# A click model on one core: two half chunks first, ten gathers a chunk, layer 0 of six chunks one group later

## The reference

```python
z0 = einsum('bid,bjd->bdij', x0, x0).reshape(B, D, F0 * F0)
cur0 = relu(einsum('bdk,kl->bld', z0, W0))            # 128 rows
next_h, direct0 = split(cur0, 2, axis=1)              # 64 and 64
z1 = einsum('bid,bjd->bdij', x0, next_h).reshape(B, D, F0 * 64)
cur1 = relu(einsum('bdk,kl->bld', z1, W1))            # 128 rows
z = sum(concat([direct0, cur1], axis=1), axis=-1)     # over d
h = relu(concat([z, dense_ctx]) @ W_top1 + b_top1)
h = relu(h @ W_top2 + b_top2);  y = h @ W_top3
```

## Time and profile before

| | us |
|---|---|
| median of three runs | 443.81 |
| the profiled run | 441.91 |
| span of its trace (first to last instruction) | 439.9 |
| PE busy | 407.8 |
| DVE busy | 347.9 |
| ACT busy | 225.7 |
| POOL busy | 285.5 |

### The profile page before, as it was taken

How to read it: one execution, slowest core, us unless ns; L and a number is a source line. 1 busy time by engine, 2 the same in 40 slices (tenths; PEclk the granted TensorE clock), 3 DMA queues, 4 the chain that set the end, 5 groups by cost and what they waited for, 6 DMA issues and landing times.

```text
span 439.9 us, 4140 instructions
## 1 busy us (share of the span) xinstructions
PE 407.8 (93%) x1490; PEld 250.4 (57%) x1490; DVE 347.9 (79%) x196; ACT 225.7 (51%) x224; POOL 285.5 (65%) x180
## 2 busy tenths in 40 slices
PE   0578699899999999999999999999999999996997
PEld 0444356446566656565756565666656565664564
DVE  0203755799999998989898989898989898999700
ACT  3114345365565647483747474747383747462422
POOL 5787878888888888888888888888888100000000
PEclk9989799999999999999999999999999999999899
DMA  8373629696959495959595977777786858570000
GB/s 282 97 180 76 133 62 217 155 208 153 213 116 213 111 208 112 212 110 216 108 220 120 200 142 171 157 178 153 176 165 157 180 138 197 127 161 0 1 0 2
DMA packets 23988, 64.03 MB, mean 146 GB/s; under 512 B 6755, under 2 KB 14904, under 8 KB 17695
## 3 DMA queue, kind: packets, MB, share of 16 engines
q1 hardware_dynamic: 17620, 60.75, 61.7%
q0 software_dynamic: 5632, 1.35, 3.1%
q10 hardware_dynamic: 715, 1.66, 1.1%
HBM read 59.88 MB, written 3.85 MB: 145 GB/s over the span
## 4 chain that ended last, share of the span: by engine, by line
PE 76%; POOL 12%; issue 5%; DVE 3%; DMA 3%; ACT 0%; DVEq 0%
PE acc L487 15%; POOL found L266 12%; PE acc L519 12%; PE acc L512 11%; PE acc L511 11%; PE acc L530 9%; PE sums L470 6%; PE acc L526 4%; PE spread L500 3%; DVE z_lo L409 3%; DMA found<-in_table_dram,rows_sb 2%; PE spread L559 2%; PE sums L550 1%; DVE z L401 1%; DMA base_sb<-in_base_dram 1%
## 5 line engine op out<-in xcount | busy, mean ns | idle before, releaser
L266 POOL DMA_INDIRECT found<-in_table_dram,rows_sb x176 | 285.3, 1621 | 56.7 <-issue 53.3
L309 ACT ACTIVATE z_hi<-z 128x2048 fp32r<-128x2048 f32 x64 | 122.4, 1912 | 83.1 <-DVE z L401 78.4
L409 DVE TENSOR_TENSOR z_lo<-z,z_hi 128x2048 fp32r<-128x2048 f32 x64 | 146.2, 2286 | 14.6 <-ACT z_hi L309 8.8
L487 PE MATMUL acc<-squares,w 128*128 128x512 f32 (+1 forms) x224 | 111.2, 614 | 0.0
L511 PE MATMUL acc<-z_hi,w_hi 128*128 128x512 f32 x256 | 106.2, 415 | 4.5 <-issue 2.3
L401 DVE TENSOR_TENSOR z<-x_wide,h 128x2048 f32<-128x2048 f32 x48 | 109.6, 2283 | 0.0
L512 PE MATMUL acc<-z_hi,w_lo 128*128 128x512 f32 x256 | 100.2, 391 | 0.0
L401 DVE TENSOR_TENSOR z<-spread,h 128x2048 f32<-128x2048 f32 x32 | 73.2, 2286 | 20.8 <-issue 17.0
L285 ACT ACTIVATE squares<-sums 128x1024 f32<-128x1024 f32 x64 | 58.4, 913 | 59.7 <-PE sums L470 45.7
L519 PE MATMUL acc<-z_lo,w_hi 128*128 128x512 f32 x256 | 83.3, 447 | 1.8 <-DVE z_lo L409 1.8
L519 PEld LDWEIGHTS acc<-z_lo,w_hi 128*128 128x128 f32 x256 | 48.5, 191 | 26.2 <-issue 15.1
(11 more groups left out here) (44 smaller groups left out, 144.5 us busy)
## 6 DMA issues: line engine op xcount, KB each, us to landing
x_wide<-x_rows SPq DMA_DIRECT2D x96, 512.0 KB
x_parts<-x_rows SPq DMA_DIRECT2D x32, 128.0 KB
found<-in_table_dram,rows_sb POOLq DMA_INDIRECT x176
x_rows<-found SPq DMA_DIRECT2D x32, 80.4 KB
w_sb<-in_w_dram SPq DMA_DIRECT2D x1, 1280.0 KB, 6.8
x_rows<-found SPq DMA_DIRECT2D x16, 73.1 KB
z<-in_select_dram ACTq DMA_DIRECT2D x1, 576.0 KB, 7.5
wt_sb<-in_wt_dram SPq DMA_DIRECT2D x1, 512.0 KB
```

The costliest lines, as they stand in the source:

```text
L266: pool.indirect_dma_start(out=found[:, b, 2, s * D:s * D + D], out_offset=None, in_=table, in_offset=bass.IndirectOffsetOnAxis(ap=rows_sb[ ...
L309: nc.scalar.activation(z_hi[:, n % RING], z[:, n % RING], ACT.Copy).then_inc(hi_done, 1)
L409: nc.vector.tensor_tensor(z_lo[:, n % RING], z[:, n % RING], z_hi[:, n % RING], ALU.subtract).then_inc(lo_done, 1)
L487: last = nc.tensor.matmul(acc0[:, :], w0[rows, t, :], squares[rows, q % RING0, a, :], start=(t == 0), stop=(t == T0 - 1))
```

## The change

- 17 chunks: two of 16 samples (256 columns), then fifteen of 32. Every instruction takes the width of its chunk.
- Gathers fetch rows in the order in which they lie in `x_rows`, 125 partitions at a time: five for the half chunks, ten for the others (160 instead of 176). The table starts are added per entry, so `base_sb` is as large as `ids_sb`. The rows go out in one transfer of 125 partitions instead of three of 39.
- The weights are loaded in another order, those of the MLP only after chunk 4's rows; `split` of chunk 0 comes earlier on ACT and DVE; the filler matmuls (`keep_busy`) are placed otherwise, and 16 stand ahead of chunk 2.
- Layer 0 of chunk c + 1 for chunks from 7 on: first sum at the end of group 4 of chunk c - 1, the next steps in groups 0, 1 and 2 of chunk c, the last contraction beside the f32 group. For chunks in `LATE` (1 to 6): first sum at the end of group 0 of chunk c, the next in groups 1 to 3, the last contraction after the high matmuls of group 3, and `h` is evicted behind it. Their `split` stands at g = 4 of chunk c - 1, on DVE behind the low part; for the others at g = 2. Chunk 2 is an exception: most of its layer 0 stands alone at the end of chunk 1, where the low part of group 4 goes ahead of the next multiply.
- On SP the way through DRAM (`bring`) of chunk c + 2 stands among the `widen` of chunk c + 1.
- The MLP of the early samples stands in groups 3 and 4 of the last chunk instead of 2 to 4.

Left out are the lines in which only the width changes.

```diff
 F = 39
 D = 16
 HALF = 64
-CB = 32
-N = CB * D
-CHUNKS = B // CB
-SETS = 3
-GP = SETS * F
-SLOTS = -(-CB // SETS)
-GW = SLOTS * D
-SET_COLS = [GW, GW, N - 2 * GW]
+
+SIZES = [16, 16] + [32] * 15
+CHUNKS = len(SIZES)
+START = [sum(SIZES[:c]) for c in range(CHUNKS)]
+WIDTH = [size * D for size in SIZES]
+N = max(WIDTH)
+
+GP = 125
+SLOTS = [-(-F * size // GP) for size in SIZES]
+SLOT0 = [sum(SLOTS[:c]) for c in range(CHUNKS)]
+GW = max(SLOTS) * D
 DENSE = 16
...
+LATE = range(1, 7)
...
-        ids_sb = sb("ids_sb", [GP, CHUNKS * SLOTS], I32)
-        base_sb = sb("base_sb", [GP, 1])
-        rows_sb = sb("rows_sb", [GP, CHUNKS * SLOTS], U32)
+        ids_sb = sb("ids_sb", [GP, sum(SLOTS)], I32)
+        base_sb = sb("base_sb", [GP, sum(SLOTS)], I32)
+        rows_sb = sb("rows_sb", [GP, sum(SLOTS)], U32)
         found = sb("found", [GP, BUFS, 3, GW])
-        x_rows = nc.dram_tensor("x_rows", (BUFS, 3, FR, N), F32, kind="Internal")
+        x_rows = nc.dram_tensor("x_rows", (BUFS, 3, FR * N), F32, kind="Internal")
...
-        hid1 = [z[:, 2, m, :] for m in range(M1 // P)]
-        hid2 = [z[:, 0, m, :] for m in range(M2 // P)]
+        hid1 = [z[:, 1, m, :] for m in range(M1 // P)]
+        hid2 = [z[:, 2, m, :] for m in range(M2 // P)]
...
             def lay_out(c):
-                b = c % BUFS
+                b, w = c % BUFS, SLOTS[c] * D
                 sp.wait_ge(found_lo_done, c + 1)
-                for s, w in enumerate(SET_COLS):
-                    start = x_rows[b, 0, 0, GW * s:GW * s + 1]
-                    sp.dma_start(bass.AP(start.tensor, start.offset, [[N, F], [FR * N, 3], [1, w]]),
-                                 found[F * s:F * s + F, b, :, 0:w]).then_inc(rows_out[b], 16)
+                start = x_rows[b, 0, 0:1]
+                sp.dma_start(bass.AP(start.tensor, start.offset, [[w, GP], [FR * N, 3], [1, w]]),
+                             found[:, b, :, 0:w]).then_inc(rows_out[b], 16)
             def place(c):
-                b = c % BUFS
-                sp.wait_ge(rows_out[b], 16 * SETS * uses(c))
+                b, w = c % BUFS, WIDTH[c]
+                sp.wait_ge(rows_out[b], 16 * uses(c))
                 for half in range(2):
-                    start = x_rows[b, half, 0, 0:1]
-                    sp.dma_start(x_parts[half:P:2, b, :].bitcast(F32),
-                                 bass.AP(start.tensor, start.offset, [[N, 2 * STEP], [STEP * N, QUADS], [1, N]])
+                    start = x_rows[b, half, 0:1]
+                    sp.dma_start(x_parts[half:P:2, b, 0:w].bitcast(F32),
+                                 bass.AP(start.tensor, start.offset, [[w, 2 * STEP], [STEP * w, QUADS], [1, w]])
...
-            sp.wait_ge(filler_in, 16)
+            sp.dma_start(w0[:, :, :], w0a).then_inc(w0_in, 16)
+            sp.dma_start(mix_sb[:, :, :], mix).then_inc(mix_in, 16)
+            sp.wait_ge(filler_in, 32)
             bring(0)
-            widen(0, 0)
-            widen(0, 1)
+            for i in range(len(WIDE)):
+                widen(0, i)
             bring(1)
-            widen(0, 2)
-            bring(2)
             for c in range(CHUNKS - 1):
-                for i in range(len(WIDE)):
-                    widen(c + 1, i)
-                if c + BUFS < CHUNKS:
-                    bring(c + BUFS)
+                widen(c + 1, 0)
+                widen(c + 1, 1)
+                if c + 2 < CHUNKS and c + 2 not in LATE:
+                    bring(c + 2)
+                widen(c + 1, 2)
+                if c + 2 < CHUNKS and c + 2 in LATE:
+                    bring(c + 2)
+                if c == 2:
+                    for dst, src in ((wt1a_sb[:, :], wt1[HALF:HALF + P, :]),
+                                     (wt1b_sb[0:HALF, :], wt1[0:HALF, :]),
+                                     (wt1b_sb[HALF:, :], wt1[HALF + P:, :]),
+                                     (wt2_sb[:, :, :], wt2), (wt3_sb[:, :], wt3), (bt1_sb[:, :], bt1),
+                                     (bt2_sb[:, :], bt2), (feat_b[HALF:, :], dense)):
+                        sp.dma_start(dst, src).then_inc(mlp_in, 16)
...
-                    pool.wait_ge(rows_out[b], 16 * SETS * uses(c - BUFS))
-                for s in range(SLOTS):
+                    pool.wait_ge(rows_out[b], 16 * uses(c - BUFS))
+                for s in range(SLOTS[c]):
+                    i = SLOT0[c] + s
                     pool.indirect_dma_start(
                         out=found[:, b, 2, s * D:s * D + D], out_offset=None, in_=table,
-                        in_offset=bass.IndirectOffsetOnAxis(ap=rows_sb[:, c * SLOTS + s:c * SLOTS + s + 1], axis=0)
+                        in_offset=bass.IndirectOffsetOnAxis(ap=rows_sb[:, i:i + 1], axis=0)
                     ).then_inc(gathered[b], 16)
...
             act.dma_start(w0b_sb, w0b).then_inc(w0_in, 16)
-            act.dma_start(mix_sb[:, :, :], mix).then_inc(mix_in, 16)
+            act.dma_start(w1_sb[:, :, :], w1).then_inc(w1_in, 16)
             act.wait_ge(select_in_done, 16)
...
+            split(0)
             act.wait_ge(w1_in, 16)
...
-            split(0)
             for d in range(ND):
                 square(d)
+            split(1)
             evict0(0)
-            split(1)
             high_part(0)
-            high_part(1)
-            square(ND)
-            square(ND + 1)
             for c in range(CHUNKS):
+                nxt = ND * (c + 1)
                 for g in range(G):
                     n = G * c + g
-                    if g == 0 and c:
+                    if g == 0 and c and c != 2:
                         evict1(c - 1)
-                    if g < 2 and c + 1 < CHUNKS:
-                        square(ND * (c + 1) + 2 + g)
-                    if g > 2 and c + 2 < CHUNKS:
-                        square(ND * (c + 2) + g - 3)
-                    if 0 < n < G * CHUNKS - 1 and is_v(n + 1):
+                    if c == 1:
+                        if g == 4:
+                            square(nxt + 1)
+                    elif c + 1 in LATE:
+                        if 0 < g < ND:
+                            square(nxt + g)
+                    elif c + 1 < CHUNKS and 1 + g < ND:
+                        square(nxt + 1 + g)
+                    if n == 2 * G - 1:
+                        evict1(1)
+                        square(nxt + 2)
+                        square(nxt + 3)
+                        evict0(2)
+                    if n + 1 < G * CHUNKS and is_v(n + 1):
                         high_part(n + 1)
-                    if g == 2 and c + 1 < CHUNKS:
+                    if c == 1 and g in (0, G - 1):
+                        split(2 if g == 0 else 3)
+
+                    if c + 1 in LATE and g == (3 if c == 1 else 0):
+                        square(nxt)
+                    if g == G - 1 and c + 2 < CHUNKS and c + 2 not in LATE:
+                        square(nxt + ND)
+                    if c != 1 and g == (3 if c + 1 in LATE else 2) and c + 1 < CHUNKS:
                         evict0(c + 1)
-                    if n == 1:
-                        split(2)
-                    if g == G - 1 and c + BUFS < CHUNKS:
-                        split(c + BUFS)
...
             dve.wait_ge(ids_in, 32)
-            nc.vector.tensor_scalar(rows_sb[:, :], ids_sb[:, :], base_sb[:, 0:1], None,
-                                    ALU.add).then_inc(rows_ready, 1)
+            nc.vector.tensor_tensor(rows_sb[:, :], ids_sb[:, :], base_sb[:, :], ALU.add).then_inc(rows_ready, 1)
+            split(0)
             dve.wait_ge(w0_in, 32)
...
-            split(0)
...
+            split(1)
             multiply(0)
-            split(1)
             for c in range(CHUNKS):
                 for g in range(G):
                     n = G * c + g
+                    if n == 2 * G - 1:
+                        low_part(n)
                     if n + 1 < G * CHUNKS:
                         multiply(n + 1)
-                    if is_v(n):
+                    if is_v(n) and n != 2 * G - 1:
                         low_part(n)
                     if n == 0:
                         reduce0(0)
-                    if n == 1:
+                    if n == G:
                         split(2)
+                    if n == 2 * G - 1:
+                        split(3)
                     if g == 1 and c:
                         reduce1(c - 1)
                     if g == G - 1 and c + 1 < CHUNKS:
                         reduce0(c + 1)
-                    if g == G - 1 and c + BUFS < CHUNKS:
-                        split(c + BUFS)
+                    if c > 1 and c + 2 < CHUNKS and g == (G - 1 if c + 2 in LATE else 2):
+                        split(c + 2)
...
-                    pe.wait_ge(multiplied, G * CHUNKS)
+                    pe.wait_ge(multiplied, G * (CHUNKS - 1) + SPREAD[-1] + 1)
...
+            pe.wait_ge(select_ready, 1)
+            keep_busy(acc0, 14)
             pe.wait_ge(w0_ready, 1)
             pe.wait_ge(mix_in, 16)
...
```

(65 more changed lines are left out.)

121 lines of the change are left out of this document (66 added, 55 removed).

## The result

The changed kernel takes 525.58 us (median of four runs, 524.98 to 526.67), the kernel before 442.38 (440.21 to 448.94, four runs): the ratio is 1.191 with a 95% interval of 1.187 to 1.195. The sign of the prediction was right (slower), the size was not: 470 was predicted, at most 482. Executions that lie far from the others at a lower granted clock (one of 527.56 us of the kernel before, at 0.75) are left out of all ratios.

The account below looks back on a forecast made before the run. TensorE was taken to bound the steady rounds at 22.88 us. Start 67.6, late rounds 34.0 + 3 x 32.6, then 268.8 to the end gave a span of 468.2; plus 2.0, 470 us, range 442 to 482.

Parts of the forecast that it names:

- Part 1: Steady rounds from chunk 6 on: same matmuls, PE still 22.88 us a chunk, ten gathers 19.3 us; change zero.
- Part 4: Late order, chunks 2 to 5: layer 0 a group later closes a loop; rounds of 32.6 us, chunk 2 34.0.
- S(2): S(c) is the start of group 0 of chunk c on PE; for chunk 2 predicted at 67.6, before 101.95.
- S(6): Start of group 0 of chunk 6 on PE, after the late rounds: predicted at 199.4, with 268.8 us to the end.
- I keep 6.05, since the two about cancel: Late rounds' way through DRAM: fewer issues against fewer DMA engines; 6.05 us kept from a range of 5.2 to 7.9.
- The clock: Late rounds: PE's idle gaps bring slow stretches, between 0 and 3.4 us a round; 0.9 taken.
- the loop: Late round through PE's steps, `h`, DVE's multiply and low part: 26.6 us, with three waits 31.7.
- Part 3: Start up to chunk 2: five gathers replace eleven, half-width instructions; group 0 of chunk 2 starts at 67.6 us.
- Part 2: The end: last group about 2.6 us earlier, against 2.1 us of layer 0 not yet done; 268.8 us instead of 269.3.
- "Worse": Rival: late rounds of 35 us and chunk 2 starting at 71, time 482 us; worse than 482 had chance 0.06.
- "Gathers set the pace again": Rival: gathers limit the rounds; set aside, 40 gathers having 25 us to spare, no price; no chance given.
- All five cases: Forecast 0.50, DRAM way hidden 0.18, bare loop 0.12, PE keeps its pace 0.14, worse than 482 us 0.06.

Follow-up runs that it names:

- the mended version: Changed kernel with the split of c + 3 back in group 4, 128 partitions, only chunks 1 and 2 late, first sum ahead of group 4's high matmuls: 436.99 us.
- The version of 448.5 us: Changed kernel with 128 partitions, chunks 1 to 3 late, split of c + 3 in group 4 (chunk 4's in groups 1 and 2 of chunk 2): 448.5 us.
- the first experiment: Changed kernel with ACT's split moved from group 2 to the end of group 1, except in late chunks: 513.5 us.

## Why the prediction was wrong, step by step

**Part 1, "Zero" for the steady round: this step failed.** It priced the matmuls and the number of gathers, and said of the rest that "only their place changes". It never followed the split that the change moves from group 4 to group 2 (it says in The change that it is moved). That one move does two things, each with a price:
- ACT's split comes to stand behind the eviction of `acc0`, which waits for PE, and DVE's split in front of four long instructions that have little slack: 26.0 instead of 23.4 us.
- Ahead of the four at the chunk's end DVE no longer pauses, and a gather is held for 9.09 us. In the changed kernel this is just covered (ten gathers with their pauses take 25.2 of 26.0 us); it is what comes next once the first is mended.

Undoing the place gives back 26.3 us in all, 25.5 of the 31.2 in this stretch (measured alone). Most of the rest is a third wait, for the square of a sum placed too late: 23.36 to 22.93, 0.43 us a round, 4.3 in ten. The cover that the prediction named, "a chunk would cost DVE's sum, still under 22.88", was the error in the reasoning: a sum of busy times under the bound says nothing of an order in which the engines wait for each other. It had said itself "If the steady round is not 22.9, part 1 is [wrong]".

"Ten need 19.3 us" was also too little: in the steady round above they take 22.21 and 3.0 us of pauses, 25.2; the mean gather is 1929 ns, before 1621. The window of the earlier trace rows shows a state of the gathers (let in at each boundary) that the change takes away, and nothing in the rows chosen hinted at it. But the trace of before held the other state once, before its third split (DVE, then POOL):

```profile
46.70 0.67 DVE L414 TENSOR_REDUCE feat_b<-direct 64x32 f32<-64x512 f32 x1
47.30 2.27 DVE L401 TENSOR_TENSOR z<-x_wide,h 128x2048 f32<-128x2048 f32 x1
49.49 2.28 DVE L409 TENSOR_TENSOR z_lo<-z,z_hi 128x2048 fp32r<-128x2048 f32 x1
```

```profile
47.96 4.69 POOL L266 DMA_INDIRECT found<-in_table_dram,rows_sb  x1 [0.30 <-issue]
```

Here no split stands behind the reduction, DVE runs on without a pause, and one gather waits out both.

**Part 4, the late rounds: mechanism right, terms too small.** 34.0 and three of 32.6 were predicted; from S(2) to S(6) 37.4 and 36.7, 35.1, 36.2 came. PE waits for DVE's low part 2.9 us in three of these rounds and 2.4 at the last boundary (about 3 predicted) and for `x_parts` 6.2, 3.2, 1.7 and 2.7. The first failed term is "I keep 6.05, since the two about cancel". The way takes 7.4 to 7.9, the upper end of the range it had itself given. With the transfer mended by splitting it in two (way near 6 us) the rounds are 32.9 to 33.5, within 1 us of the 32.6. The clock is the second term, and the larger one in the round shown: 0.9 us were taken. That round has 0.82 and, after the mending, 0.93; its first sum comes 8.7 us after its start (7.1 predicted, 1.6 late), and from there to the end of the first contraction it takes 6.8 us (123.40 to 130.16), where a sum, a square, a sum and a contraction at full clock make 3.7. The longer wait seems to bring its own slow stretch (the contraction at half clock stands right behind it), so that a term and its consequence were both short.

On the transfer the prediction weighed the rule of the Trainium skill, "DMA: Bandwidth & Descriptors", section "Why a DMA increments its semaphore by 16 and not by 1": the number of DMA engines is the largest up to 16 that divides the slowest dimension of both sides, so 5 for 125 partitions. The runs agree in the order of sizes: 3.94 to 4.46 us for 125 partitions, 2.14 to 2.16 for 128, 1.98 to 2.92 for 112 and 13. How many engines carried each is not shown here. The estimate of 32.7 for the loop that hung on it was still too low: the transfer took more than the 2.9 us of engine time, and the clock's loss came on top.

The claim that the low part on DVE is the link of the loop fell with the run that put it first.

**Part 3, the start: 9.75 us too short.** The order was right, the small terms too small, and the delay grows on the way: the split of chunk 0 on ACT at 14.22 (12.2 predicted), its first sum at 20.63 (18.8), that of chunk 1 at 34.70 (29.9), that of chunk 2 at 60.56 (52.6), S(2) at 77.35 (67.6). The way out and back took 5.9 and 6.0 us for the two half chunks, as predicted, and 7.5 for chunk 2. The first 1.0 us is lost ahead of all gathers: the two index tables are added up at 4.71, in the kernel before at 3.16, and the prediction took 0.6 for that.

```profile
4.71 0.33 DVE L456 TENSOR_TENSOR rows_sb<-ids_sb,base_sb 125x160 uint32<-125x160 int32 x1 [4.71 <-DMA base_sb<-in_base_dram]
```

With 128 partitions this stands at 3.29, the split at 11.91, the first sum at 17.35, and chunk 2's first multiply is reached at 67.21 instead of 74.77: 7.6 us less, in the loading of the two tables, in the gathers (0.95 us against 1.21) and in the transfers. (Among the versions that leave 125 partitions and the transfer as they are that multiply lies between 73.1 and 75.4.) The prediction took the gather's time for unchanged although it rises from 117 to 125 partitions; no row showed that. It isn't a matter of more work: 128 take 0.95.

**Part 2, the end, held to within 1 us.** From S(16) to the end of the span it is 41.0 us in the changed kernel and in the version with 128 partitions, 40.9 in the one with the waits mended; 40.0 was predicted. From S(6) on the mended version takes 434.1 - 164.32 = 269.8 us, the kernel before from S(5) 439.9 - 170.44 = 269.5; the prediction had 268.8 and 269.3.

**The sum, set right.** 525.6 less 26.3 (the split's place, measured alone), less 4.3 (the square, from the rounds of another version) and less 22.1 (128 partitions, measured alone) is 472.9, beside the 470 predicted. The three were not run together in this form, so that is an account, not a measurement. The version of 448.5 us comes near it: it has the first and the third and three late chunks fewer, each some 10 us; 448.5 + 30 - 4.3 is 474.

**The rivals.** None came. "Worse" (rounds of 35 and S(2) = 71) came nearest to the late rounds (35 to 37) and the start (77.4), with 0.06 on it, and even that kept 268.8 us from S(6) on. All five cases shared Part 1, so the range could not hold what went wrong there: with one term of ten rounds in every case, its error had to be a rival of its own. "Gathers set the pace again" had been put aside with 25 us to spare; they do set it as soon as the round falls to 23.4 (chunks 11 to 14 of the first experiment).

## What to carry to other kernels

When an instruction is moved along an in-order engine, ask what it will wait for in its new place and what is queued behind it, even where all busy times stay the same; here that one move cost 26 us, and the busy times of PE and DVE in a round had not changed by 1 us. Where ten or more rounds share a term, give its failure a case of its own. Between two bounds of an unknown transfer, do not let two guesses cancel: choose by the shape; here 125 partitions were slower than 128 in the gather and in the transfer.
